# An attention and expert layer on one core: one pool of four PSUM banks for transposes and projections, and two steps issued a unit later

## What is computed

```python
xn = layernorm(x)
q, k, v = heads(xn @ Wq.T + bq), heads(xn @ Wk.T + bk), heads(xn @ Wv.T + bv)
s = q @ k.T / sqrt(D) + causal + alibi
att = (softmax(s) @ v) @ Wo.T + bo
p = softmax(xn @ gate_w.T); topw, sel = top_k(p, 2); topw /= topw.sum(-1)
g, u = split(xn @ w1[e].T)                      # for each expert e
ffn = sum_e combine[:, e] * ((silu(g) * u) @ w2[e].T)
out = x + att + ffn
```

## Time and profile before

| | |
|---|---|
| median of 3 runs | 1620.87 us (1618.1 to 1623.33) |
| profiled execution, time | 1621.4 us |
| profiled execution, span from first to last instruction | 1619.6 us |
| mean granted TensorE clock | 0.974 |

### The profile page before, as it was taken

One profiled execution on the slowest core, in us unless ns is written; L12 is line 12 of the kernel. 1 busy time (PEld: TensorE's weight loads), 2 busy tenths in 40 slices (PEclk: granted clock), 3 DMA queues, 4 the chain that ended last, 5 costly groups with the idle time before them and its releaser, 6 DMA issues.

```text
span 1619.6 us, 35530 instructions
## 1 busy us (share of the span) xinstructions
PE 1471.8 (91%) x12763; PEld 894.1 (55%) x12763; DVE 1043.0 (64%) x2494; ACT 888.4 (55%) x2020; POOL 567.1 (35%) x595
## 2 busy tenths in 40 slices
PE   3799998998998999999899798999789999999995
PEld 1465565555555555555555466665356656556662
DVE  6688787675878777777888978777243333333331
ACT  4378676664777776776866465677212222222221
POOL 3111033121113222112311224131216777777775
PEclk9899999998999999999999999999999999999998
DMA  7243531433333254442314242235687888888884
GB/s 256 66 130 105 146 92 52 106 107 105 109 109 92 91 141 130 137 130 86 109 45 123 78 120 62 67 89 179 241 228 118 137 125 139 138 138 126 134 142 46
DMA packets 171350, 193.28 MB, mean 119 GB/s; under 512 B 87536, under 2 KB 121072, under 8 KB 171056
## 3 DMA queue, kind: packets, MB, share of 16 engines
q1 hardware_dynamic: 143760, 151.67, 34.8%
q0 software_dynamic: 26128, 37.24, 14.0%
q10 hardware_dynamic: 1296, 2.11, 0.3%
HBM read 93.45 MB, written 53.74 MB: 91 GB/s over the span
## 4 chain that ended last, share of the span: by engine, by line
PE 69%; DVE 11%; issue 6%; DMA 4%; ACT 4%; SPq 4%; POOL 2%; POOLq 0%; DVEq 0%; ACTq 0%
PE S L1187 16%; PE T L1110 11%; PE O L1126 7%; PE S L1067 5%; PE S L1099 5%; PE M L1067 5%; PE M L1218 4%; PE O L1218 4%; DVE arena L1492 4%; SPq L944 3%; PE M L1149 2%; PE S L1084 2%; PE M L1084 2%; DVE arena L1503 1%; PE T L1202 1%
## 5 line engine op out<-in xcount | busy, mean ns | idle before, releaser
L1492 DVE CUSTOM_DVE_ANT_0 arena<-S,cF,nsl 128x1024 f32<-128x1024 f32 (+7 forms) x512 | 413.1, 811 | 69.7 <-PE S L1099 47.3
L1682 ACT ACTIVATE arena<-arena,mneg 128x1024 f32<-128x1024 f32 (+7 forms) x512 | 395.3, 772 | 60.2 <-DVE mneg L1492 59.5
L1110 PE MATMUL T<-cF,arena 128*128 128x128 f32 x2304 | 366.7, 280 | 64.6 <-ACT arena L1696 35.9
L1696 ACT ACTIVATE arena<-T 128x512 f32<-128x512 f32 (+3 forms) x536 | 242.4, 466 | 252.1 <-PE T L1110 249.2
L1110 PEld LDWEIGHTS T<-cF,arena 128*128 128x128 f32 x2304 | 268.6, 143 | 166.2 <-issue 50.5
L1187 PE MATMUL S<-arena 128*128 x1704 | 269.1, 315 | 10.5 <-issue 10.5
L1835 POOL DMA_INDIRECT out<-arena x142 | 221.9, 1562 | 106.8 <-ACT arena L1742 60.4
L1187 PEld LDWEIGHTS S<-arena 128*128 128x128 f16 x1704 | 167.4, 98 | 109.1 <-issue 11.8
L1503 DVE COPY arena<-T 128x512 f32<-128x512 f32 (+3 forms) x296 | 151.7, 516 | 112.6 <-PE T L1110 111.2
L1126 PE MATMUL O<-arena 128*32 128x128 f32 (+1 forms) x3328 | 212.6, 331 | 7.4 <-DVE arena L1523 6.3
L1099 PE MATMUL S<-arena 96*128 96x512 f16 (+3 forms) x768 | 212.9, 332 | 3.3 <-DMA arena<-arena 1.7
(11 more groups left out here) (187 smaller groups left out, 1819.4 us busy)
## 6 DMA issues: line engine op xcount, KB each, us to landing
arena<-arena SPq DMA_DIRECT2D x192, 128.0 KB, 2.4
arena<-in_w1T SPq DMA_DIRECT2D x64, 352.0 KB, 3.4
arena<-in_x SPq DMA_DIRECT2D x64, 256.0 KB, 3.4
w_d<-arena SPq DMA_DIRECT2D x32, 352.0 KB, 2.9
arena<-w_d SPq DMA_DIRECT2D x16, 704.0 KB, 7.1
arena<-in_w2T SPq DMA_DIRECT2D x32, 256.0 KB, 2.9
out<-arena SPq DMA_DIRECT2D x32, 256.0 KB, 3.2
xn_d<-arena SPq DMA_DIRECT2D x24, 256.0 KB, 2.0
```

What stands on the lines that cost most here:

```text
L1110: tp = pe.transpose(z[:, (c - c0) * P:(c - c0 + 1) * P], ring[u % 4][:, c * P:(c + 1) * P], idf)
L1492: dve.tensor_tensor_reduce(ring[r][:, 0:w], SBK[o.bank["score", u]][:, 0:w], rel[:, S - w:S], nsl[:, hh:hh + 1], 3.0e38, ALU.add, ALU.min, ...
L1682: act.activation(ring[r][:, 0:w], ring[r][:, 0:w], ACT.Exp, bias=mneg[:, m:m + 1], scale=-1.0, accum_out=rs[:, k, c:c + 1]).then_inc(sems[ ...
L1696: act.activation(PT[k][:, h, to_:to_ + gap * (c1 - c0 - 1) + 1:gap, :], TB[o.bank["tr", u, i]][:, 0:n].rearrange("p (c n) -> p c n", n=P), ...
```

## The change

The T and M banks become one pool of four, B. `borrow` gives a step the free bank that was given back longest ago, `give` returns it when its emptying step is put into the list. Transposes of probabilities, of normalised tiles, and all projections borrow from it. In the expert phase the transposes use two of the four under the name X. `scaled` is called twice for a value pass: the first time it adds only `rsb`, the second time, an iteration later, `a32` and `aT`. In `ln_steps`, tile i gets `xn` in step i, `xnh` and `xnl` in step i+1, and its transposition in step i+4 in place of i+3, with eight steps in place of seven. All other hunks replace `MBK` and `TB` by `PB` and `leave("M", ...)` by `give(...)`.

```diff
-        self.size = {"S": 2, "T": 2, "O": 1, "M": 2, "Y": 2}
+        self.size = {"S": 2, "O": 1, "X": 2, "Y": 2}
...
+        self.since, self.owner = dict.fromkeys(range(4), 0), {}
...
+    def borrow(self, *key):
+
+        i = min((i for i in range(4) if i not in self.owner), key=lambda i: self.since[i])
+        self.owner[i] = key
+        self.bank[key] = i
+        self.emptied[key] = self.tenant.get(("B", i), [])
+
+    def give(self, key, *steps):
+        i = self.bank[key]
+        del self.owner[i]
+        self.since[i] = len(self.steps)
+        self.tenant[("B", i)] = list(steps)
...
     def take_m(*key):
         if len(later) > 1:
             flush()
-        o.take("M", *key)
+        o.borrow(*key)
...
     def ln_tile(b, half, i):
         add("xn", b, half, i)
+        ln_split(b, half, i)
+
+    def ln_split(b, half, i):
         add("xnh", b, half, i)
         add("xnl", b, half, i)
...
-            o.take("T", "tr", u, i)
+            o.borrow("tr", u, i)
             add("tr", u, i)
             yield
             en = lighter((c1 - c0) * P)
             add("pt", u, i, en, sem="pt" + en)
             o.count["pt", u, i] = o.count["pt", u, i, en]
-            o.leave("T", ("tr", u, i), ("pt", u, i))
+            o.give(("tr", u, i), ("pt", u, i))
...
     def scaled(u):
+        b, g, j = unit(u)[:3]
+        if tpv[u]:
+            tpv[u] = False
+            add("rsb", u)
+            return
         tpv.pop(u)
-        b, g, j = unit(u)[:3]
-        add("rsb", u)
         add("a32", u)
         o.leave("O", ("pv", u), ("a32", u))
...
-            for i in range(7):
-                if i > 2:
+            for i in range(8):
+                if i > 3:
                     yield from lock()
                     held[0] = False
-                    ln_turn(b, half, i - 3)
+                    ln_turn(b, half, i - 4)
                 if i < 4:
-                    ln_tile(b, half, i)
-                if i == 5 and half == 0 and b:
+                    add("xn", b, half, i)
+                if 0 < i < 5:
+                    ln_split(b, half, i - 1)
+                if i == 6 and half == 0 and b:
                     ln_load(b, 1)
-                if i < 6:
+                if i < 7:
                     yield
...
-    s1, m1 = o.tenant["S", 1], o.tenant["M", 1]
+    s1, m1 = o.tenant["S", 1], o.tenant["B", 3]
     o.tenant["S", 1] = s1 + m1
-    o.tenant["Y", 0], o.tenant["Y", 1] = o.tenant["O", 0], o.tenant["M", 0]
-    o.turn["T"] = 0
+    o.tenant["Y", 0], o.tenant["Y", 1] = o.tenant["O", 0], o.tenant["B", 2]
+    o.tenant["X", 0], o.tenant["X", 1] = o.tenant["B", 0], o.tenant["B", 1]
...
-    MBK = [ps("M", [P, 512], F32), GU[1][:, 512:1024]]
-    YB = [OB, MBK[0]]
+    MB = ps("M", [P, 512], F32)
+    PB = [*TB, MB, GU[1][:, 512:1024]]
+    YB = [OB, MB]
```

More of the change, by code:

```diff
@@ L195, in rest @@
             o.count["xt", b, half, i] = o.count["xt", b, half, i, en]
-            o.leave("M", key, ("xt", b, half, i))
+            o.give(key, ("xt", b, half, i))
         later.append(rest)
@@ L210, in rest @@
             add("lg", b)
-            o.leave("M", ("gate", b), ("lg", b))
+            o.give(("gate", b), ("lg", b))
         later.append(rest)
@@ L226, in rest @@
             add("qk32", b, g, qk, half)
-            o.leave("M", key, ("qk32", b, g, qk, half))
+            o.give(key, ("qk32", b, g, qk, half))
             load["act"] += 0.7
@@ L253, in rest @@
             add("vsb", b, g, half)
-            o.leave("M", key, ("vsb", b, g, half))
+            o.give(key, ("vsb", b, g, half))
         later.append(rest)
@@ L406, in routing @@
         add("route", 12)
[L407 removed]
+        o.give(("rank",), ("route", 12))
         yield
@@ L529, in widest @@
         flush()
-        o.take("M", "gmax", what, part)
+        o.borrow("gmax", what, part)
         add("gmax", what, part)
@@ L533, in widest @@
         add("gtop", what, part)
-        o.leave("M", ("gmax", what, part), ("gtop", what, part))
+        o.give(("gmax", what, part), ("gtop", what, part))
         yield
@@ L1018, in tensor @@
                     on.wait_ge(*at(*s))
-                tz = MBK[o.bank[step]][:, :].bitcast(F16)
+                tz = PB[o.bank[step]][:, :].bitcast(F16)
                 k = half_place(*key)
@@ L1025, in tensor @@
                 b, part = key
-                z = MBK[o.bank["gate", b]]
+                z = PB[o.bank["gate", b]]
                 if part == 0:
@@ L1042, in tensor @@
                 what, part = key
-                z = MBK[o.bank["gmax", what, part]]
+                z = PB[o.bank["gmax", what, part]]
                 c, n = (LW, 3) if what == "w" else (LWO, 1)
@@ L1056, in tensor @@
                 b, g, qk, half, third = key
-                z = MBK[o.bank["qk", b, g, qk, half]]
+                z = PB[o.bank["qk", b, g, qk, half]]
                 if third == 0:
@@ L1072, in tensor @@
                 b, g, half, i = key
-                z = MBK[o.bank["v", b, g, half]]
+                z = PB[o.bank["v", b, g, half]]
                 if i == 0:
@@ L1107, in tensor @@
                     on.wait_ge(*at(*s))
-                z = TB[o.bank[step]]
+                z = PB[o.bank[step]]
                 for c in range(c0, c1):
@@ L1166, in tensor @@
                     on.wait_ge(*at(*s))
-                z = MBK[o.bank[step]]
+                z = PB[o.bank[step]]
                 for k in range(8):
@@ L1378, in vector @@
                 tt = half * 4 + i
-                tz = MBK[o.bank["xtp", b, half, i]][:, :].bitcast(F16)
+                tz = PB[o.bank["xtp", b, half, i]][:, :].bitcast(F16)
                 on.wait_ge(*at("xtp", b, half, i))
```

28 lines of the change are left out of this document (14 added, 14 removed).

## The result

| | before | after |
|---|---|---|
| median | 1619.78 us (1618.1 to 1623.33, 4 runs) | 1640.58 us (1636.14 to 1644.58, 4 runs) |
| ratio | 1 | 1.012, 95% interval 1.0091 to 1.0148 |
| profiled execution, time | 1621.4 us | 1642.63 us |
| span, mean granted clock | 1619.6 us, 0.974 | 1640.8 us, 0.96 |

The change makes the kernel 1.2% slower. The forecast of 1599 was wrong in direction, and the range ended at 1626.

What follows compares the result with a forecast made beforehand. PE was taken to bound the kernel almost everywhere, with 71.8 us idle in attention's thousand. From 1621.4 us: pool -46, scaling +29, split 0, attention's end +1, clock -6, together -22, so 1599; range 1566 to 1626.

Steps and rivals of the forecast that it cites:

- Part 1, the pool: Attention's transposes with four shared banks: 62.8 us of PE's copy waits, 17 kept, 46 us gained, bounds 63 and 20.
- the waits only move: Rival, chance 0.15: VectorE's bursts stop PE elsewhere in attention; 20 us gained by the pool, 20 lost by scaling, 1621 within 5.
- Part 2, the scaling: Output scaling a unit later holds the only O bank at 32 of 64 boundaries: 29 us lost, bounds 0 and 54.
- The three boundaries: Three sampled starts of value passes after long passes: mean wait 1.3 us against 0.46, 0.85 more each.
- it costs PE: Claim that O-bank waits stop PE, as value matmul, next transposes and scores queue behind them: 29 us lost.
- Part 3, the split: Normalised tile's split a step later: ScalarE stops standing 20.2 us, PE gains 0 us, bounds -3 and +2.
- Part 4, the end of attention: Last scaling and second last output projection tile a unit later, before the expert phase: cost 1.0 us, bounds 0 and 3.
- Part 5, the clock: Granted clock 0.98 in attention loses about 20 us; shorter waits return 6 us, bounds 0 and 12.
- the clock falls: Rival, 0.03: shorter, more scattered idle moments lower attention's granted clock from 0.98 to 0.95; PE loses 30 us more, 1635.
- a clock under 0.96: Listed sign that the forecast is wrong; it had expected the granted clock to rise a little above 0.98.
- The O bank becomes the lock: Rival, chance 0.15: PE arrives early at 32 value-pass boundaries and waits for late VectorE, 54 us; 1630 to 1641.
- the 1582: Forecast's sum by the skill's bank rotation advice alone, with the whole 62.8 us of attention's copy waits gone.

## Why the forecast was wrong, step by step

**Part 1, the pool (46 us and 6 of clock).** The kept waits for copies were put at 17 us; the changed kernel has 17.8. But that number is not a gain: with the pool alone, copies fell by 31 us, and 17 of these came back as O and score waits. The rival "the waits only move" named this mechanism, and I took score waits of 1.4 us today as evidence against it, which they are not: a wait that is always met by an earlier one does not show. The term was 46 and measured 12.

**Part 2, the scaling (29 us).** The added wait was nearly right: O waits of 6.6 + 29 = 36 were forecast and 36.4 came alone, 44.8 with the pool. They stand where it said: 47.1 of the changed kernel's 54.2 us behind passes of 8 and 7 pieces. The three boundaries were a fair sample. The step that failed is the last one, "it costs PE": each microsecond of O wait was booked as a microsecond of time. Alone the kernel lost 5.5 us, with the pool 2.6. The traces show two things that pay for the O waits: the waits for copies that would have come next shrank (by 16 us alone, by 9 with the pool), and VectorE's 27.4 us of waits for the reciprocals are gone. How much each paid was not measured apart. Where the late scaling was kept to the boundaries with room, it was worth 16 us with the pool and 5 without. I had given VectorE's relief no gain of its own.

The errors of parts 1 and 2 nearly cancel, by luck: together they were forecast at -17 us, and pool and late scaling together measured -9.6 (0.9941). What is left of the miss is part 3.

**Part 3, the split (0 us, bounds -3 and +2).** This is the step that failed and turned the sign. Alone it cost 10.5 us, on top of pool and late scaling 29 (1.012 against 0.9941). I followed the moved instructions on VectorE, ScalarE and GpSimd and wrote that "the gate and projections of the next batch start two units later", and priced it without asking who has a deadline there. The first score of a batch waits for stacks that come behind those projections, behind a shared lock, and on SyncE's queue behind a store that must land. None of this was in the rows: before, the stacks had six units of room in the list, of which 1.9 to 3.6 us were left when they had landed, and PE never waited for them after the first batch. The late split with the late scaling takes four of the six units. With the next batch's normalisation started four units earlier all 29 us were back (0.9932). Of these, the stacks' unit alone explains 4 to 11. The rest is spread over the store in front of them, the list products and O waits, in shares that stay open.

**Part 4, the end of attention (1 us).** From the last score to the end of the span it was 472.9 us before and 469.8 after. No loss is seen there.

**Part 5, the clock (6 us gained).** It went the other way: 109 us at the lower level (1.2 GHz) in attention, 61 before. In the trace of before eleven of twelve falls in attention lie at a wait of 1.6 us or more, in the changed kernel all nineteen do: waits for the stack, for O up to 5.0 us, for list products. Not each such wait has a fall beside it: two of 13 in the trace of before and five of 26 in the changed kernel have no fall within 5 us. Part of the lost clock falls into the waits themselves. Attention less PE's idle time is 1001.3 us before and 1005.4 after, so 4 of the 25.5 us that attention grew are outside of idle time. The clock of 0.95 in 100 to 1100 us is the number of the rival "the clock falls", but not its mechanism: the falls lie at long waits, not at scattered short ones. By the Trainium skill (TensorE: Matmul & The Clock Gate, A second HAM failure mode: psum-queue depth-cycling) cycling through banks can make the clock change between its levels; this case does not show it, since the pool alone cycles through the same four banks and has 68 us at the lower level, 61 before. Of the signs of being wrong in the forecast, "a clock under 0.96" is the one that came.

**The rivals.** "The O bank becomes the lock" gave the right time by luck. Its O waits came as priced (1.7 x 32 = 54, measured 54.2), but it took each of them for lost time and the pool's gain for 35 to 46 us; with the measured 12 its own sum would be 54 - 12 + 1 = 43 us slower. With the O waits all left in place, but the stacks issued two units earlier and ahead of a store, the loss is gone. The Trainium skill (Perfetto Trace Analysis, Optimizing Tensor Performance, Matmuls) advises rotating over banks. The pool alone, at 1609, is faster, as that advice says; the 1582 that I had worked out by it, with all waits for copies gone, did not come.

## What to carry to other kernels

A step moved by one slot in a list with shared locks and in-order queues moves everything behind it: find, on each engine and on the DMA queue, the next consumer with a deadline, and count its room, in steps and in microseconds, before pricing the move at nothing. Wait time is not a sum: removing a wait at a bank shows the next one on the same late engine, so a gain booked from a list of waits needs the slack to the next dependence on that engine (here 12 of 46 us stayed). When several small reorderings go in together, measure the pairs: here the parts cost or gained 12 us at most and one pair cost 31.

## What was not expected of the hardware

Nothing new of the chip was needed to explain the result. The granted clock fell mostly at single waits of PE of 1.6 us and more, and attention had 44 to 109 us at the lower level. A 128x128 fp32 transpose on PE had a median of 273 ns and a maximum of 477 in the kernel before; the 44 of 2304 that lie wholly in stretches at 0.50 have a median of 421 ns, so the two levels are seen there too.
